# Four operations a chunk in a delta-rule scan, with w copied to PSUM, joint reciprocal roots, and the steps of five engines put in another order

## The reference

```python
def step(Sm, inp):
    qi, ki, vi, bi = inp
    Sk = jnp.einsum('bhkv,bhk->bhv', Sm, ki)
    Sm = Sm + bi[..., None, None] * ki[..., :, None] * (vi - Sk)[..., None, :]
    oi = jnp.einsum('bhkv,bhk->bhv', Sm, qi)
    return (Sm, oi)
# then, on tokens: h = hidden + o @ Wo; y = rmsnorm(h); h = h + silu(y @ Wg) * (y @ Wu) @ Wd
# x3 = layernorm(x2 + h)
# a, b = x3 @ w1 * s1, x3 @ w2 * s2;  g = silu(a) * b;  m = gelu(g @ h1 * t1);  n = gelu(m @ h2 * t2)
# x4 = layernorm(x3 + n @ w3 * s3)
```

## Time and profile before

| | us |
|---|---|
| median of 3 runs | 1372.63 (1371.8 to 1373.66) |
| profiled execution | 1367.92 |
| its span | 1366.2 |
| busy in the span: PE, DVE, ACT, POOL | 1170.0, 926.2, 623.3, 453.3 |
| first operation of the scan | 848.52 |
| granted clock of TensorE, mean | 0.944 |

### The profile page before, as it was taken

One profiled execution on the slowest core, in us unless ns is written; L12 is line 12 of the kernel. 1 busy time (PEld: TensorE's weight loads), 2 busy tenths in 40 slices (PEclk: granted clock), 3 DMA queues, 4 the chain that ended last, 5 costly groups with the idle time before them and its releaser, 6 DMA issues.

```text
span 1366.2 us, 19874 instructions
## 1 busy us (share of the span) xinstructions
PE 1170.0 (86%) x6173; PEld 616.5 (45%) x6173; DVE 926.2 (68%) x2401; ACT 623.3 (46%) x1194; POOL 453.3 (33%) x466
## 2 busy tenths in 40 slices
PE   5989889999899998989896751178999999999997
PEld 2434355453554544635444430134555545455453
DVE  3536536657587677776775577988988988898321
ACT  2071743736737447375373410213464454545642
POOL 3031311212333143232333233236446445544510
PEclk8999999999999999999999885579999999999999
DMA  3212030130321414114213168121020220200000
GB/s 99 82 47 71 1 109 9 48 94 33 109 65 42 131 32 134 47 29 138 55 35 67 25 149 200 48 49 44 14 65 19 47 65 8 57 24 8 24 8 8
DMA packets 85756, 79.91 MB, mean 58 GB/s; under 512 B 42800, under 2 KB 63408, under 8 KB 83632
## 3 DMA queue, kind: packets, MB, share of 16 engines
q1 hardware_dynamic: 85680, 79.01, 21.6%
HBM read 43.17 MB, written 35.00 MB: 57 GB/s over the span
## 4 chain that ended last, share of the span: by engine, by line
PE 50%; DVE 25%; ACT 10%; issue 9%; POOL 4%; DMA 1%; SPq 0%; ACTq 0%; DVEq 0%; POOLq 0%
PE ps L1305 10%; PE ps L954 5%; PE ps L1288 5%; DVE arena L1808 4%; ACT arena L1442 4%; PE ps L991 4%; PE ps L923 4%; ACT arena L1404 3%; PE ps L957 3%; PE ps L964 3%; PE ps L980 2%; DVE arena L2075 2%; PE ps L1058 2%; DVE ps L2070 2%; DVE arena L2073 2%
## 5 line engine op out<-in xcount | busy, mean ns | idle before, releaser
L1808 DVE TENSOR_REDUCE arena<-ps 128x4 f32<-128x512 f32 (+2 forms) x192 | 197.8, 1044 | 89.4 <-PE ps L957 86.3
L1305 PE MATMUL ps<-arena,late 128*128 128x512 f32 x512 | 224.5, 592 | 0.0
L1404 ACT ACTIVATE arena<-ps 128x512 f32<-128x512 f32 (+2 forms) x200 | 109.7, 567 | 232.6 <-PE ps L923 105.4
L1442 ACT ACTIVATE arena<-ps 128x1024 f32<-128x1024 f32 (+3 forms) x256 | 169.9, 711 | 30.6 <-PE ps L980 29.5
L753 POOL TENSOR_SCALAR_AFFINE_SELECT arena<-arena 128x512 f32<-128x512 f32 x128 | 82.9, 650 | 291.9 <-ACT arena L1442 290.4
L964 PE MATMUL ps<-mask_qk,ident_b 128*128 128x512 bf16 x505 | 137.6, 390 | 31.2 <-DVE arena L2087 31.1
L1305 PEld LDWEIGHTS ps<-arena,late 128*128 128x128 f32 x512 | 96.2, 190 | 115.8 <-issue 114.1
L1591 ACT ACTIVATE arena<-ps,f_s 128x512 f32<-128x512 f32 x128 | 85.2, 688 | 102.9 <-PE ps L1305 93.9
L1288 PE MATMUL ps<-arena,late 128*128 128x512 f32 x256 | 116.6, 609 | 7.8 <-ACT arena L1591 7.3
L848 POOL TENSOR_TENSOR arena<-arena 128x512 f32<-128x512 f32 x64 | 81.7, 1276 | 120.8 <-DVE slot_T L2104 76.5
L1404 ACT ACTIVATE arena<-ps,arena 128x128 f32<-128x128 f32 (+1 forms) x128 | 62.3, 528 | 124.5 <-DVE arena L1835 49.3
(11 more groups left out here) (186 smaller groups left out, 1960.7 us busy)
## 6 DMA issues: line engine op xcount, KB each, us to landing
qr<-q_rep SPq DMA_DIRECT2D x8, 1024.0 KB, 5.6
kr<-k_rep SPq DMA_DIRECT2D x8, 1024.0 KB, 7.9
scan_d<-late SPq DMA_DIRECT2D x56, 138.0 KB, 3.0
arena<-scan_d SPq DMA_DIRECT2D x12, 552.0 KB, 7.2
q_rep<-hilo SPq DMA_DIRECT2D x24, 256.0 KB, 3.3
k_rep<-hilo SPq DMA_DIRECT2D x24, 256.0 KB, 3.8
proj_d<-arena SPq DMA_DIRECT2D x8, 768.0 KB, 5.1
late<-proj_d SPq DMA_DIRECT2D x8, 768.0 KB, 4.5
```

Source lines behind the costliest of these rows:

```text
L1305: last = pe.matmul(ps[:, ring2.bank(f"{n}{c}"), :], w[:, k, c * P:(c + 1) * P], src[:, k, :], start=(k == 0), stop=(k == HC - 1))
L1404: return act.activation(dst, src(ps[:, bank, :]), func, **kw)
L1442: act.activation(prob[:, gg % 2, 2 * pr:2 * pr + 2, p_off[jt]:p_off[jt] + w], ps[:, bank:bank + 2, 0:w], ACT.Exp).then_inc(p_taken, 1)
L1808: v.tensor_reduce(heads[:, 2 * pr:2 * pr + 2, gs[0]:gs[-1] + 1], ps[:, at:at + 2, 0:len(gs) * w].rearrange("p q (n w) -> p q n w", w=w), X ...
```

## The change

- A chunk has four operations. The copies of w (ACT, `place_wv`) go to PSUM beside u, a quarter at a time, and -v into the ninth column of the tile that the first product writes; so the first reduction gives u with its sign in one go. The state lies in the fifth column of the tile that the second product writes, so the second reduction gives the new state. The first product now reads w in PSUM and the state in SBUF.
- `place_wv` for quarter q+2 stands in ACT's queue behind `keep_history` of quarter q (`place_behind`). DVE waits for `w_placed` and `v_negated` at each quarter's first chunk.
- The inverse roots of the RMS norm and of the last layer norm are taken in one run of eight operations (`roots` over `st_both`).
- `out_products` of the second half go by quarters. In one step two of the gates of the last MLP stand before those of the last quarter.
- TensorE: project_o behind m0, turn_h behind m2 (in the first such step behind m2 and m3), turn_x3 in the middle of last_out, and fewer idle matmuls.
- DVE: other counts (AT_Y 4, AT_H 26, AT_X 56, AT_S 60, AT_FIRST 44, of 64), two scan operations between sums in place of one, `add_x4` behind the sums; in step 1 `norm_x3` behind operation 56 and not behind the scan.
- ACT: `square_h` before `apply_x4`, the copy of hT before the four of m; in step 1 quarter 3 is kept only in step 2, behind the first two of `take_ab`.

```diff
+        live_u = [ps[:, 6 + k, 0:QUARTER * HD * CH].rearrange("p (c v j) -> p c v j", v=HD, j=CH) for k in range(2)]
+        live_w = [ps[:, 6 + k, QUARTER * HD * CH:2 * QUARTER * HD * CH].rearrange("p (c j d) -> p c j d", j=CH, d=HD) for k in range(2)]
+        w_s = [c2.take(QUARTER * HD, CH, HD + 1) for _ in range(2)]
+        k_u = [c2.take(QUARTER * HD, HD, CH + 1) for _ in range(2)]
+        live = [tile[:, :, :, CH].rearrange("p (c v) d -> p c v d", v=HD) for tile in k_u]
+        v_neg = [tile[:, :, :, HD].rearrange("p (c v) j -> p c v j", v=HD) for tile in w_s]
+        st_both = slot_T[:, 256:256 + 64].rearrange("p (k a b) -> p k a b", k=2, a=8)
...
# POOL
+            def step(scan, mlp, last, h, ahead=None, gated=0):
...
+                    for q, n in ((0, 2), (2, 1), (3, 1)):
+                        if q == 3 and ahead is not None:
+                            gate_ab(ahead, 0)
+                            gate_ab(ahead, 1)
                         for r in range(CH):
-                            out_products(scan, h, half, r)
+                            out_products(scan, h, q, n, r)
...
# TensorE
+            def last_out(t, turn, beside):
+                by_token("y", turn, hid_n, f_w3, a2_act, CREDIT + A2.emptied("n0", t) - 1, beside).then_inc(a2_ready, 1)
+            def step(mlp, last, h, before, o_at=0, h_at=2):
...
+                elif mlp is not None:
+                    pe.wait_ge(om_summed, CREDIT + 5)
+                    idle_matmuls(32, 5)
+                for k in range(HC):
+                    if last is not None:
+                        layer_m(last, turn, k)
+                    if mlp is not None and k == o_at:
+                        project_o(mlp, turn)
+                        if last is None:
+                            idle_matmuls(24, 5)
+                    if mlp is not None and k == h_at:
+                        turn_h(mlp, turn)
...
-                    last_out(last, turn)
-                if mlp is not None:
-                    if last is None:
-                        idle_matmuls(56, 5)
+                    last_out(last, turn, (lambda: turn_x3(mlp, turn, 1 - h)) if mlp is not None else None)
+                elif mlp is not None:
+                    idle_matmuls(26, 5)
                     turn_x3(mlp, turn, 1 - h)
-                    if last is not None:
-                        idle_matmuls(3, ring2.bank("n2"))
...
+            now = step(1, 0, 0, now, 2, 3)
...
# ACT
+            def place_wv(t, h, q):
+                act.wait_ge(sc_loaded[h], CREDIT + (t - h) * 16 + 48)
+                cs = slice(q * QUARTER, (q + 1) * QUARTER)
+                wc = s_wu[h].rearrange("p (c j) w -> p c j w", j=CH)
+                act.activation(live_w[q % 2], wc[:, cs, :, 0:HD], ACT.Copy).then_inc(w_placed, 1)
+                wc = s_wu[h].rearrange("p (c j) w -> p c w j", j=CH)
+                act.activation(v_neg[q % 2], wc[:, cs, HD:2 * HD, :], ACT.Copy, scale=-1.0).then_inc(v_negated, 1)
...
                 if last is not None:
                     take_n(last, 2)
                     take_n(last, 3)
+                if scanned is not None and last is not None:
+                    place_behind(scanned, h, 3, more)
                 if mlp is not None:
                     apply_x3(mlp, 1 - h)
...
# DVE
+                    if at == 0:
+                        v.wait_ge(w_placed, CREDIT + t * 4 + c // QUARTER + 1)
+                    yield o.mark(v.tensor_tensor(w_s[half][:, rows, :, 0:HD],
+                                                 live_w[half][:, at, :, :].unsqueeze(1).broadcast_to([P, HD, CH, HD]),
+                                                 live[half][:, at, :, :].unsqueeze(2).broadcast_to([P, HD, CH, HD]), ALU.mult))
+                    if at == 0:
+                        v.wait_ge(v_negated, CREDIT + t * 4 + c // QUARTER + 1)
+                    yield o.mark(v.tensor_reduce(now_u, w_s[half][:, rows, :, :], X, ALU.add, negate=True))
+                    yield o.mark(v.tensor_tensor(k_u[half][:, rows, :, 0:CH], now_u.unsqueeze(2).broadcast_to([P, HD, HD, CH]),
                                                  kt[:, c, :, :].unsqueeze(1).broadcast_to([P, HD, HD, CH]), ALU.mult))
-                    yield o.mark(v.tensor_reduce(ku_sum, k_u, X, ALU.add))
                     if at == QUARTER - 1:
                         v.wait_ge(hist_kept, CREDIT + t * 4 + c // QUARTER)
-                    yield o.mark(v.tensor_tensor(after[:, (c + 1) % QUARTER, :, :], now[:, at, :, :], ku_sum, ALU.add))
+                    yield o.mark(v.tensor_reduce(after[:, (c + 1) % QUARTER, :, :], k_u[half][:, rows, :, :], X, ALU.add))
...
+                if early_x3:
+                    upto(AT_X)
+                    norm_x3(mlp, 1 - h, Order(v, ln3_done, DVE_LN, mlp, CREDIT))
                 if scanned is not None:
-                    upto(AT_S)
+                    upto(AT_S if mlp is not None else AT_FIRST)
...
-AT_Y, AT_N, AT_H, AT_S = 4, 18, 34, 84
+AT_Y, AT_H, AT_X, AT_S, AT_FIRST = 4, 26, 56, 60, 44
```

More of the change, by code:

```diff
@@ L1288, in by_hidden, with by_token @@
                 return pe.matmul(ps[:, ring2.bank(use), :], w, src, start=True, stop=True)
-            def by_token(use, turn, hid, w, done, first):
+            def by_token(use, turn, hid, w, done, first, beside=None):
                 ring2.wait_free(pe, use, *turn)
                 for j in range(4):
+                    if j == 2 and beside is not None:
+                        beside()
                     for c in range(HC):
@@ L1380, in _ @@
             now = step(0, None, 1, {})
-            now = step(1, 0, 0, now)
+            now = step(1, 0, 0, now, 2, 3)
             with pe.Fori(0, 2) as i:
@@ L1641, in keep_history, with place_behind, step @@
                 act.activation(u_c[h][:, cs, :, :], live_u[q % 2], ACT.Copy).then_inc(hist_kept, 1)
-            def step(scanned, mlp, last, done, h):
+            def place_behind(t, h, q, more=True):
+                if q < 2:
+                    place_wv(t, h, q + 2)
+                elif more:
+                    place_wv(t + 1, 1 - h, q - 2)
+            def step(scanned, mlp, last, done, h, more=True, behind=None):
                 if last is not None:
@@ L1646, in step @@
                         take_ab(last, c)
+                        if c == 1 and behind is not None:
+                            keep_history(behind, 1 - h, 3)
+                            place_behind(behind, 1 - h, 3)
                 if scanned is not None:
                     keep_history(scanned, h, 0)
+                    place_behind(scanned, h, 0)
+                if mlp is not None:
+                    square_h(mlp)
                 if done is not None:
@@ L2117, in add_x4, with moments_x4, step @@
                 v.tensor_tensor(y4, arrived2(A2, "y", t).rearrange("p (b d) -> p b d", d=D), x3[h], ALU.add).then_inc(a2_dve, 1)
[L2119 removed]
+            def moments_x4(t, o):
                 v.wait_ge(a2_dve, CREDIT + A2.emptied("y", t))
[L2121 to L2125 removed]
+                moments(o, y4, bn4, st4, 4)
+                o.step(v.tensor_scalar(st4[:, 2, :], st4[:, 2, :], RSQRT_SCALE * LN_EPS, None, ALU.add))
+            def step(scanned, mlp, done, h, early_x3=False):
                 further = upto = lambda n: None
@@ L2131, in step @@
                     upto = lambda n: advance(o_scan, steps, max(n - o_scan.n, 0))
-                def order(done, per, t, beside):
-                    o = Order(v, done, per, t, CREDIT)
-                    if beside:
-                        o.between = lambda: further(1)
-                    return o
                 upto(AT_Y)
-                if done is not None:
-                    add_x4(done, 1 - h)
                 if mlp is not None:
@@ L2157, in step @@
                 further(DVE_SCAN)
-                if mlp is not None:
-                    norm_x3(mlp, 1 - h, order(ln3_done, DVE_LN, mlp, False))
+                if mlp is not None and not early_x3:
+                    norm_x3(mlp, 1 - h, Order(v, ln3_done, DVE_LN, mlp, CREDIT))
             step(0, None, None, 0)
-            step(1, 0, None, 1)
+            step(1, 0, None, 1, True)
             step(2, 1, None, 0)
```

128 lines of the change are left out of this document (58 added, 70 removed).

## The result

The median after is 1363.62 us against 1372.22: 8.6 us faster by the medians, and a ratio of 0.9933 (0.9916 to 0.995), which is 6.9 to 11.5 us. The forecast was 19.5. In a second measurement of the same kernel, beside more runs of before, it was 1358.48 against 1372.59, a ratio of 0.99 (0.9873 to 0.9927).

A forecast was written before the change was run, and what follows sets the result against it. DVE's scan was taken to bound the second part up to the first gates_ab, a nearly full TensorE from tile 1's to tile 7's. Gains 8.2 + 11.3 = 19.5 us gave a median of 1353, range 1345 to 1364.

The forecast's parts named there:

- The chunk, 2.00: DVE's scan chunk, four operations in place of six: 2.00 us in place of 2.35, with ends 1.93 and 2.17.
- 3.1 us for each 0.1: Before gates_ab of tile 1 some 31 chunks lie on the path, so 0.1 us more a chunk costs 3.1.
- Up to ab 0: From scan 0 to the start of gates_ab of tile 0: norm_x3 at 922.3 for 936.74, 14.4 us gained.
- ab 0, 7.48 later as before: gates_ab of tile 0 starts 7.48 us after norm_x3 starts, as before the change, at 929.8.
- Given back by ab 1: Between the starts of gates_ab of tiles 0 and 1, 6 us lost again; 8.2 stay gained at 988.6.
- A step after ab 1, 51.8: Steps between starts of gates_ab, tiles 1 to 7: five of 51.8 us, one 50.8; 309.8 against 321.14, 11.3 gained.
- slack of 4.1: DVE's work in a later step was put at 47.7 of 51.8 us; one loop end, 3.2, fits inside.
- the floor: Rival on TensorE's floor: apply_x3 is not late, later steps take 50.8 us, total 1346.5; chance 0.18.
- The hopping operands: Rival: word-by-word reads and writes in the scan cost the upper bound, 2.17 us a chunk, total 1358.5; chance 0.09.
- Late copies: Rival: ACT's copies of w and v come late, DVE waits at each quarter, 1 us a step, total 1359; chance 0.06.
- A clock that falls in each step: Rival: TensorE's clock falls behind the gap before x3T, 3.4 us each, seven times, total 1376.6, slower; chance 0.05.

The follow-up runs named there:

- experiment 6: Four edits of the changed kernel: product 1 reads adjacent words, 1354.74 us; state at pitch 6 and 8, 1357.94; sources exchanged, 506.5 from scan 0; w in SBUF, 1377.2.
- experiments 2 and 4: Changed kernel with GpSimd's scan 1 products held until norm_x3 is done (2), 1358.52 us; or spread, first quarter's before its gates, third's behind norm_x3 (4), 1352.75.
- experiment 5: Changed kernel with TensorE's gaps filled by idle matmuls, 48 for 26 before x3T of tile 0 and 16 new before hT of tile 1: 1358.01 us.
- experiment 7: Changed kernel with ACT's copies of w and v of quarter 3 moved behind x3T: 1360.77 us.

## Why the prediction was wrong

- *The chunk, 2.00*: 2.13, inside the bounds, near the upper end (2.17). The failure is the choice: I took L1929 as proof that a source read word by word is free. By the prediction's own 3.1 us for each 0.1 the 0.13 cost 4.0 before ab 1, and experiment 6 bears the rate out: 5.9 for 0.19. Other terms of the start were too long by about as much (next point), so that this miss hardly shows in the sum; that is luck. L1929 reads by twos, one word from each of two rows 16 apart, then the next word of both; the scan reads eight words in one walk at a pitch of five. The Trainium skill, "Vector Engine (DVE) Microarchitecture Reference", section 5.2, gives 1.73 ns an element for a source that hops at each and 1.05 for adjacent ones, 0.68 more (an estimate from that page, whose hop is 4 KiB); the runs come near, (614 - 423)/256 = 0.75. The same section has a stream that alternates between two regions at the full rate, which is nearer to what L1929 does; no run here tells whether that is why.
- *Up to ab 0*: norm_x3 started at 73.5, and 73.8 was forecast. That is in part luck. TensorE's product set the start, but the chunk lies on the way to that product: with the state adjacent norm_x3 starts at 69.4 (experiment 6). Against this residual_h came only 1.3 late, where 0.13 in each of 22.5 chunks are 2.9; and from the gates to norm_x3 it took 13.9 for the 15.0 forecast, as the clock fell for less of the gates (8.52 for 9.61). Then comes **the step that failed**: "ab 0, 7.48 later as before". That length holds norm_x3's 4.4, which was read where GpSimd stood. In the earlier trace rows most of GpSimd's wait was for `ln3_done` (L2104), so before the change norm_x3 had no products beside it, and moving it to operation 56 put it among them: 8.7 for 4.4, shown by experiments 2 and 4. In the Trainium skill it stands under "SBUF — State Buffer", "Who interferes with whom": a VectorE operation with two SBUF inputs and a GpSimd operation that reads SBUF exclude each other for a whole instruction. The ends shown above agree, in norm_x3 and in the 44 products of experiment 6.
- *Given back by ab 1*: 6.2 were forecast, with 1.5 for the clock; ab 0 to ab 1 took 62.2 against 58.8. The gap of 3.9 at hT was there as forecast (4.2). Its clock fall was priced, but not the one of ab 0, which norm_x3's delay made: gates 9.13 and 9.35 for 7.13 each, 4.2 in all; filling both gaps brought 4.0 (experiment 5). The delay also made GpSimd's last quarter late (DVE waited 3.4). Together 4.4 up to ab 0 and 3.4 from there are the 7.8 missing at ab 1.
- *A step after ab 1, 51.8*: 309.5 in all against 309.8, but two misses cancel in it. Three steps took 51.5, one 51.0 and the last 50.9; the gap before x3T, forecast 1.0, was 0.65, by ACT's copies as said (experiment 7). The step with the loop's end took 53.1, with hT late by 1.34. Its loop end was to lie inside VectorE's slack of 4.1. But a scan took 2.1 more than forecast, and norm_x3 5.2 to 5.6 in place of 4.4 in every one of these steps but the last. With the state adjacent this step takes 51.7 (experiment 6).
- *Rivals*: the floor was there to be had but for the loop's end (steps of 50.9 to 51.0, 307.9 in all), though not in this kernel. The hopping operands were nearly at their upper bound, as the rule of the Trainium skill had them. Late copies: the only long wait for them is that before the first product of scan 0, 4.1 us, where the kernel before waited 3.8 for the load itself. A clock that falls in each step: no. It fell in three gates, those of tile 0 (8.52, as before the change), gates_ab of tile 0 and the gates of tile 1, all before ab 1; from there on all gates take 7.03.

## What to carry to other kernels

A duration moves with its place only if what stands beside it moves too: before a small VectorE chain is moved, look at which engine its old place kept quiet. Here a delay of 4 us in front of TensorE cost twice, itself and then in the clock of the matmuls behind it; idle matmuls there won back 4 us with the delay still in place. And a row that is to price an access must walk through memory as the new code does; that it hops too is not enough.

## What the runs showed of the hardware

- Two VectorE sources in SBUF beside a GpSimd operation: a product on 4 words took 1.26 us for 0.17 and ended 0.03 after GpSimd's operation, one on 256 words 1.75 for 0.62 and ended 0.49 after it. Beside norm_x3 GpSimd's operations kept their length (1.28); beside the products of 256 words they took up to 1.78 for 1.27.
- A source in SBUF at a pitch of 5, 6 or 8 words costs 612 to 617 ns for 256 elements, adjacent words 423; writing runs of four at a pitch of 5 (L2115) costs nothing.
- ACT's copy of the state takes 666 ns from the strided tile in SBUF, 383 from PSUM before.
- The first part, the same instructions in every kernel here, ended between 846.7 and 856.1 us, counted to the first operation of scan 0 in fourteen executions.
- TensorE's clock after a gap of much the same length differed by execution: the gates of tile 0 took 7.13 behind gaps of 1.68, 1.75 and 1.87 us (experiments 6, 7 and 5) and 8.5 to 8.8 behind 1.42, 1.52 and 1.91 (experiments 6 and 2, changed kernel).
